# A pair of attention layers on one core: the final steps of two units on GpSimd, and the last unit in strided halves

## The reference

```python
for layer in (L0, L1):
    h = group_norm(x, 32 groups, eps) * gain + bias
    q, k, v = h @ Wq + bq, h @ Wk + bk, h @ Wv + bv     # 64 x 64 each, per position
    s = softmax((q @ k.T) * 64**-0.5)                   # 1024 x 1024 for each image
    x = x + (s @ v) @ Wo + bo
```

## Time and profile before

| what | us |
|---|---|
| time, median of 3 runs | 185.82 (185.78 to 186.77) |
| span of the profiled execution, first to last instruction | 184.0 |
| median less span, what lies around it | 1.8 |
| TensorE busy, share of the span | 174.6, 95% |
| VectorE | 138.3, 75% |
| GpSimd | 121.8, 66% |
| ScalarE | 100.4, 55% |

### The profile page before, as it was taken

How to read it: one execution, slowest core, us unless ns; L and a number is a source line. 1 busy time by engine, 2 the same in 40 slices (tenths; PEclk the granted TensorE clock), 3 DMA queues, 4 the chain that set the end, 5 groups by cost and what they waited for, 6 DMA issues and landing times.

```text
span 184.0 us, 3303 instructions
## 1 busy us (share of the span) xinstructions
PE 174.6 (95%) x1223; PEld 93.5 (51%) x1223; DVE 138.3 (75%) x208; ACT 100.4 (55%) x137; POOL 121.8 (66%) x81
## 2 busy tenths in 40 slices
PE   7778899999999999999999999999999999999993
PEld 4435545555525644455535645555535555456661
DVE  2799987779887687859875787769875588386763
ACT  3479367606656376436666476527656554466500
POOL 5265017996799929996699949996799939705000
PEclk9999999999999999999999999999999999999999
DMA  5544100500016000420025000500025100110111
GB/s 154 189 100 98 34 2 0 114 4 2 0 34 142 2 0 14 102 60 0 0 54 122 0 4 20 136 18 0 5 59 115 61 0 21 37 61 7 50 57 57
DMA packets 7103, 8.89 MB, mean 48 GB/s; under 512 B 1656, under 2 KB 4144, under 8 KB 7088
## 3 DMA queue, kind: packets, MB, share of 16 engines
q1 hardware_dynamic: 6080, 7.84, 16.9%
q10 hardware_dynamic: 1008, 0.86, 1.6%
HBM read 1.58 MB, written 1.05 MB: 14 GB/s over the span
## 4 chain that ended last, share of the span: by engine, by line
PE 82%; DVE 13%; DMA 1%; issue 1%; POOL 0%; ACT 0%; DVEq 0%; POOLq 0%
PE ps_attn L887 27%; PE ps_max L817 9%; DVE part_max L588 8%; PE ps_scores L855 8%; PE ps_scores L871 7%; PE ps_scores L857 7%; PE ps_scores L859 7%; PE ps_scores L796 3%; PE ps_misc L804 2%; PE ps_attn L894 2%; PE ps_misc L900 2%; DMA xs<-x_dram 1%; PE ps_misc L894 1%; DVE quarter_rden L628 1%; PE ps_misc L831 1%
## 5 line engine op out<-in xcount | busy, mean ns | idle before, releaser
L313 POOL TENSOR_TENSOR prob_sum<-prob_sum,probs 128x1024 f32<-128x1024 f32 x41 | 97.5, 2377 | 29.0 <-ACT probs L441 16.8
L588 DVE TENSOR_REDUCE part_max<-ps_max 128x2 f32<-128x1024 f32 x60 | 73.4, 1224 | 26.3 <-PE ps_max L818 25.8
L441 ACT ACTIVATE probs<-ps_scores 128x1024 f32<-128x1024 f32 x62 | 61.0, 1025 | 46.1 <-PE ps_scores L872 45.4
L887 PE MATMUL ps_attn<-probs,vals 128*64 128x512 f32 x224 | 54.5, 605 | 0.0
L887 PEld LDWEIGHTS ps_attn<-probs,vals 128*64 128x64 f32 x224 | 13.5, 136 | 27.8 <-issue 19.2
L871 PE MATMUL ps_scores<-q_row,ones_r 64*128 64x512 f32 x62 | 24.5, 396 | 0.5 <-ACT q_row L423 0.5
L872 PE MATMUL ps_scores<-q_row,ones_r 64*128 64x512 f32 x62 | 24.6, 396 | 0.0
L817 PE MATMUL ps_max<-back,front 64*128 64x512 f32 x31 | 13.9, 449 | 2.3 <-DVE part_max L588 1.4
L817 PE MATMUL ps_max<-cross,front 64*128 64x512 f32 x29 | 14.6, 505 | 0.3 <-DVE part_max L588 0.3
L818 PE MATMUL ps_max<-cross,back 64*128 64x512 f32 x29 | 14.6, 505 | 0.0
L818 PE MATMUL ps_max<-front,back 64*128 64x512 f32 x31 | 14.0, 450 | 0.0
(11 more groups left out here) (157 smaller groups left out, 365.7 us busy)
## 6 DMA issues: line engine op xcount, KB each, us to landing
cross<-front SPq DMA_DIRECT2D x16, 128.0 KB, 2.3
cross<-back SPq DMA_DIRECT2D x16, 128.0 KB, 2.3
rden<-quarter_rden SPq DMA_DIRECT2D x44, 32.0 KB, 1.8
xs<-x_dram SPq DMA_DIRECT2D x4, 256.0 KB, 4.6
out_dram<-xs SPq DMA_DIRECT2D x3, 256.0 KB, 2.0
rden<-quarter_rden ACTq DMA_DIRECT2D x12, 32.0 KB, 1.9
q_row<-max_rows SPq DMA_DIRECT2D x14, 2.0 KB
layer<-layers_dram SPq DMA_DIRECT2D x1, 194.5 KB, 2.7
```

Of the source, the lines that this page charges most:

```text
L313: pool.tensor_tensor(total[:, :], total[:, :], probs[t][:, :], ALU.add).then_inc(added, 1)
L441: act.activation(probs[t][:, :], scores_buffer(u, t)[:, :], ACT.Exp, scale=SCALE).then_inc(exp_done, 1)
L588: dve.tensor_reduce(part_max[u % 2][:, at:at + 2 * JS + 1:2 * JS], ps[:, :].rearrange("p (g n) -> p g n", g=2), AX.X, ALU.max, negate=True ...
L887: mm = pe.matmul(ps_attn[half * C:(half + 1) * C, :], v, probs[t][:, cols], start=(t == 0), stop=(t == TILES - 1))
```

## The change

It touches only the end of the program, in five places.

1. The final steps of units 5 and 6 become `finish` on GpSimd. Unit 5's comes behind tile 5 of unit 6, unit 6's at the very end of GpSimd's queue. The stores of those units wait for `final_done` instead of `tail_final`.
2. GpSimd adds tiles 2 and 3 of unit 7 (`TAIL_ADDS` is (4, 2)). VectorE collects the rest in `late_sum`: tile 4 plus tile 5, plus tile 6, plus `prob_sum`, plus tile 7. TensorE then sums one tile over its rows, one group in place of two.
3. The two halves of unit 7 are strided: half c takes every other block of 128 columns (`split`), not the first or second 256. With that, one reciprocal piece serves one half.
4. `spread_last` writes the two halves to different PSUM buffers and raises its semaphore for each; ScalarE copies each as its own instruction; the spread of both comes between `values_last(0)` and `values_last(1)`. ScalarE's copy waits for unit 6's multiply (`normed`), and `finish_last(0)` for unit 5's final step.
5. TensorE's order: `denominators(6)` comes one values tile earlier, values tile 7 of unit 6 behind score tile 3, values tile 1 of unit 7 behind the last score tiles, and values tile 4 ahead of the last sums.

```diff
-    TAIL_ADDS = (4, 1)
+    TAIL_ADDS = (4, 2)
...
+        def split(columns, c):
+            return columns.rearrange("p (k c n) -> p k c n", k=2, c=2)[:, :, c, :]
...
+        def last_rden(c):
+            return (ps_max, scores_buffer(LAST, TILES - 2))[c][:, 0:HALF // 2]
...
                 sp.wait_ge(quarter_done, 2 * u + 2)
-                if u == LAST - 1:
-                    sp.wait_ge(tail_normed, 1)
-                elif u:
+                if u:
                     sp.wait_ge(normed, u)
...
                 for t in range(2, 2 + pool_adds(w)):
                     add(w, t)
-                    if t == 5 and 0 < w < LAST - 1:
+                    if t == 5 and 0 < w < LAST:
                         finish(w - 1)
+            finish(LAST - 1)
...
-            act.wait_ge(last_spread, 1)
-            act.wait_ge(tail_normed, 2)
-            act.activation(rden[:, :], ps_max[:, HI], ACT.Copy).then_inc(last_rden, 1)
+            act.wait_ge(normed, LAST)
+            for c in range(2):
+                act.wait_ge(last_spread, c + 1)
+                act.activation(split(rden[:, :], c), last_rden(c), ACT.Copy).then_inc(last_copied, 1)
+            act.wait_ge(tail_final, 2)
+            act.dma_start(split(out[B - 1], 1), split(xs[:, slot(LAST + B)], 1)).then_inc(stored, 16)
...
+            def add_late(step):
+                if step == 1:
+                    dve.wait_ge(exp_done, TILES * LAST + 6)
+                    dve.wait_ge(tail_added, 1)
+                    first, second = probs[4], probs[5]
                 else:
+                    first, second = late_sum, (probs[6], prob_sum[LAST % 2], probs[7])[step - 2]
+                    dve.wait_ge(late_added, step - 1)
+                    if step == 3:
+                        dve.wait_ge(added, added_count(LAST, 3))
+                    else:
+                        dve.wait_ge(exp_done, TILES * LAST + (7 if step == 2 else 8))
+                dve.tensor_tensor(late_sum[:, :], first[:, :], second[:, :], ALU.add).then_inc(late_added, 1)
...
-            finish_tail(LAST - 2)
             pair_tail(LAST - 1)
             add_tail(LAST - 1)
             first_add(LAST)
             reciprocal(LAST - 1, 0)
             reciprocal(LAST - 1, 1)
-            for t in range(3, TILES - 1):
-                add_late(t)
-            finish_tail(LAST - 1)
+            for step in range(1, 5):
+                add_late(step)
...
-                pe.wait_ge(late_added, TILES - 4)
-                quarter_sums(ps_max[:, HALF:HALF + HALF // 2], prob_sum[LAST % 2], True, False)
-                pe.wait_ge(exp_done, TILES * UNITS)
-                quarter_sums(ps_max[:, HALF:HALF + HALF // 2], probs[TILES - 1], False, True).then_inc(den_mm, 1)
+                pe.wait_ge(late_added, 4)
+                quarter_sums(ps_max[:, HALF:HALF + HALF // 2], late_sum, True, True).then_inc(den_mm, 1)
...
             values(LAST - 1, 6)
-            values(LAST - 1, 7)
             pe.wait_ge(max_staged, UNITS)
             denominators(LAST - 1)
             scores(LAST, 3)
+            values(LAST - 1, 7)
             scores(LAST, 4)
             scores(LAST, 5)
             pe.wait_ge(quarter_done, 2 * LAST)
             values(LAST, 0)
-            values(LAST, 1)
             scores(LAST, 6)
             scores(LAST, 7)
+            values(LAST, 1)
             values(LAST, 2)
             values(LAST, 3)
+            values(LAST, 4)
             denominators_last()
-            values(LAST, 4)
             values(LAST, 5)
+            values_last(0)
             spread_last(0)
             spread_last(1)
-            values_last(0)
             values_last(1)
```

More of the change, by code:

```diff
@@ L250, in store @@
                 unit = UNITS - B + image
[L251 to L254, removed]
+                sp.wait_ge(final_done, unit + 1)
                 sp.dma_start(out[image], xs[:, slot(unit + B)]).then_inc(stored, 16)
             def store_last():
-                at = (LAST + B) * HALF
-                sp.wait_ge(tail_final, 3)
-                sp.dma_start(out[B - 1, :, 0:HALF // 2], xs[:, at:at + HALF // 2]).then_inc(stored, 16)
+                sp.wait_ge(tail_final, 1)
+                sp.dma_start(split(out[B - 1], 0), split(xs[:, slot(LAST + B)], 0)).then_inc(stored, 16)
             for u in range(2):
@@ L445, in copy_attn @@
                 if u >= 2:
[L446 to L449, removed]
+                    act.wait_ge(final_done, u - 1)
                 act.activation(attn[u % 2][:, :], ps_attn[:, :], ACT.Copy).then_inc(attn_copied, 1)
@@ L649, in add_tail @@
                 dve.tensor_tensor(total[:, :], total[:, :], late_sum[:, :], ALU.add).then_inc(tail_added, 1)
[L651 to L655, removed]
-                else:
-                    dve.wait_ge(late_added, t - 3)
-                dve.tensor_tensor(total[:, :], total[:, :], probs[t][:, :], ALU.add).then_inc(late_added, 1)
@@ L669, in finish_last @@
             def finish_last(c):
-                a, at = attn[LAST % 2], (LAST + B) * HALF
-                cols = slice(c * HALF // 2, (c + 1) * HALF // 2)
-                dve.wait_ge(last_rden, 1)
-                dve.wait_ge(tail_final, 1)
+                a = split(attn[LAST % 2][:, :], c)
+                dve.wait_ge(last_copied, c + 1)
                 dve.wait_ge(pv_mm, TILES * UNITS - 1 + c)
-                dve.tensor_tensor(a[:, cols], (ps_attn, ps_misc)[c][:, 0:HALF // 2], rden[:, cols], ALU.mult).then_inc(tail_normed, 1)
@@ L676, in finish_last @@
-                dve.wait_ge(tail_normed, 3 + c)
+                if c == 0:
+                    dve.wait_ge(final_done, LAST - 1)
+                values = (ps_attn, ps_misc)[c][:, 0:HALF // 2].rearrange("p (k n) -> p k n", k=2)
+                dve.tensor_tensor(a, values, split(rden[:, :], c), ALU.mult).then_inc(tail_normed, 1)
+                dve.wait_ge(tail_normed, 1 + c)
                 dve.wait_ge(x_biased, UNITS)
-                dve.tensor_tensor(xs[:, at + cols.start:at + cols.stop], a[:, cols],
-                                  xs[:, LAST * HALF + cols.start:LAST * HALF + cols.stop],
+                dve.tensor_tensor(split(xs[:, slot(LAST + B)], c), a, split(xs[:, slot(LAST)], c),
@@ L891, in half_values @@
             def half_values(t, v, c):
-                for half in range(2):
-                    at = half * HALF + c * HALF // 2
+                for half, cols in enumerate(halves()):
                     mm = pe.matmul((ps_attn, ps_misc)[c][half * C:(half + 1) * C, 0:HALF // 2], v,
-                                   probs[t][:, at:at + HALF // 2], start=(t == 0), stop=(t == TILES - 1))
+                                   split(probs[t][:, cols], c), start=(t == 0), stop=(t == TILES - 1))
                 return mm
@@ L930, in spread_last @@
                         q = 2 * n + k
-                        at = k * HALF // 2 + c * P
-                        mm = pe.matmul(ps_max[n * C:(n + 1) * C, at:at + P],
+                        mm = pe.matmul(last_rden(c)[n * C:(n + 1) * C, k * P:(k + 1) * P],
                                        pick[:, q * C:(q + 1) * C], quarter_rden[:, c * P:(c + 1) * P],
                                        start=True, stop=True)
-                if c:
-                    mm.then_inc(last_spread, 1)
+                mm.then_inc(last_spread, 1)
             def setup(n):
```

13 lines of the change are left out of this document (1 added, 12 removed).

## The result

The changed kernel took 190.56 us (median of 4 runs, 189.87 to 191.12) against 186.22 us of the kernel before in the same runs: 1.0231 times as long, 95% interval 1.0193 to 1.0268. The forecast was 188.1, the range ended at 188.9. A second series gave 189.92 against 186.34, ratio 1.0195 (1.0153 to 1.0238). The direction and the main mechanism were forecast; the rise, 4.3 us where 2.3 were forecast, was nearly double.

A forecast was written before the change was run, and what follows sets the result against it. TensorE's gapless last stretch and VectorE's finishing pairs were taken as the bound. End 181.72 us, plus 0.4 for the additions and 2.0 for GpSimd's hold, gave 184.1 against 181.83 (+2.3): forecast 188.1 us, range 185.9 to 188.9.

The forecast's parts named there:

- TensorE's work: TensorE's final stretch: one group of sums removed (0.43 us), one order change added (0.35 us), 0.08 to 0.10 us saved.
- VectorE's additions: Unit 7's four late additions: the fourth needs tile 7 and ends late, so TensorE's last sums wait 0.4 us.
- the switches of the new order: TensorE's order in units 6 and 7: one more change between scores and values, costing 0.35 us.
- GpSimd's steps: GpSimd's multiply and add of unit 6, due at 174.0 us, hold VectorE's third and fourth late additions; 2.0 us lost.
- step 2: Second of VectorE's four late additions for unit 7, running when GpSimd's multiply comes due, laid out at 173.1 to 174.3 us.
- Rivals 1 and 2: VectorE's late additions: first, only one is held, 187.1 us, chance 0.15; second, no contention with GpSimd, 186.1 us, chance 0.15.
- rival 3: TensorE's last sums: late_sum ready by 176.53 us, GpSimd holds nothing, so not slower; 185.7 us, chance 0.10.
- The strides, 0 for the stores: Last stores in 512-byte instead of 1 KB pieces: landing taken as unchanged, 0 us, at worst 1.7 us more.
- rival 4: Last stores: as forecast, but small pieces land 0.5 to 1 us later; 188.9 us, chance 0.05.

The follow-up runs named there:

- the pairs: Kernel storing x unchanged, without the computation; VectorE and GpSimd start one instruction each at one signal, ten pairs; GpSimd's addition 3.38 us beside VectorE's two-input one, 2.34 alone.
- the filler in the gap: Changed kernel plus four matmuls with unused results ahead of TensorE's last group of sums; 189.03 us, ratio 1.0149 to the kernel before.
- gated: Changed kernel with GpSimd's final step of unit 6 waiting for VectorE's fourth late addition; 187.50 us, ratio 1.0057 to the kernel before.
- reordered kernel: Changed kernel with GpSimd's unit 6 step held back, TensorE's old order of scores and values, and prob_sum added second; 186.28 us, ratio 0.9998 to the kernel before.
- block stores: On top of the reordered kernel, one transfer for each 128-column block of the last unit, two per queue; 186.17 us, ratio 1.0003 to the kernel before.

## Why the prediction was right and where it failed

**TensorE's work**: right, where the clock is full. The sums begin when VectorE's fourth addition ends, and the groups have the sizes of the earlier trace rows.

**VectorE's additions, 0.4 us late by themselves**: right; 0.43 in the run with the step held back. The wait and the switches of the new order (0.35 in the prediction) make 0.78; taking both back gave 0.77 in the traces and 1.2 in the medians.

**GpSimd's steps, 2.0 us**: right in place and size. The two additions took 0.95 longer each, 1.9; holding the step back gave them their 1.23 again. The hold works in the other direction too: GpSimd's L319 is 1.66 instead of 1.28, since step 2 was running when it came due, and in the pairs it is GpSimd that waits. The Trainium skill ("SBUF — State Buffer", section "SBUF: two separate sides") has the rule that whichever of the two starts first keeps the shared ports for its whole instruction; these rows agree with it in both directions. Rivals 1 and 2 fall by the same rows; rival 3 as well.

**The strides, 0 for the stores**: wrong. The step that failed is "I take 0, since the nearest row is the same store". It was not the same store: the new one has twice as many pieces, each half as long. It lands after 2.2 us instead of 1.7, and takes 0.66 us to issue instead of 0.36. That was rival 4, given 0.05; its 0.5 us alone would have left the time at 188.6, inside the range.

**What had no term at all**: the clock. What took the time out of the range is work at the lower clock, and the step that failed is the price of the gap. The prediction read that the clock was full in all slices and that TensorE had no gap, forecast a gap of 2.4 us, and priced it at its own length ("End: 181.72 + 2.4 = 184.1"). The gap came, 2.32 us. In one of the two traces of the changed kernel the matmuls behind it ran at 1.2 GHz and the stretch took 1.6 us more; in the other they ran at 2.4 GHz. With the filler in the gap no execution of four was at 0.991 or below, where nine of ten had been, and the median fell by 0.9 us. That this fall happens in most executions is inferred from those means, not seen in traces.

**The sum**: in the first trace 1.0 us at the start of the program, 2.3 for the additions and their wait and 0.5 for the stores make the 3.8 of the span. The 1.0 is a fall of the clock in a stretch that the change leaves alone, which nothing in the trace of the kernel before announced. The one execution with full clock has a span of 186.9 against 184.0, 2.9, where 2.3 + 0.5 = 2.8; that it fits to 0.1 is partly luck, since spans vary by more at full clock (183.7 to 184.8 in the kernel before). The medians of the two series differ by 4.3 and 3.6; the 1.5 and 0.8 that are over fit the clock, but no run splits them by execution.

Left open: in how many executions the clock fell at the start and in how many at the end, what the three at 0.987 had, whether the other 0.4 us between the gated and the reordered kernel is the clock, why one queue's block stores land at 2.1 and whole pieces once at 2.9, and why the first series is 0.6 us above the second.

## What to carry to other kernels

Before work is moved to GpSimd, look at what VectorE runs beside it at that moment: here two-input additions in SBUF and GpSimd's own took turns, and reciprocals from PSUM did not. Price a forecast gap on TensorE with the clock behind it, as a second case beside the gap's own length, and where a gap can't be closed, try to fill it. Price a store that is the last thing in a program by its pieces too, not only by its bytes: the 0.37 us by which the reordered kernel ended earlier on VectorE were eaten by its stores. And before a mean clock is blamed on a change, look in the trace where it fell; here one mean, 0.991, stood for two different places.

## What the runs showed of the hardware

A VectorE addition of two SBUF tiles (1.23 us) delayed GpSimd's addition by 1.04 us; a single-input VectorE instruction on float32 in SBUF, 1024 elements in 0.69 us, delayed it by 0.50. A GpSimd memset of 0.95 us beside a two-input addition delayed neither, and with one input in PSUM GpSimd's addition kept its 2.34 us. The delay shows in the records as a longer instruction (2.17 us for 1.23), not as idle time.

Behind a TensorE wait of 2.32 us the granted clock was 0.50 in one trace of the changed kernel and 1.00 in another; behind one of 0.43 us it was 1.00 in both traces that have it (the step held back, with strided and with whole stores).

A 128 KB store to HBM in 512-byte pieces took 2.2 to 2.3 us to land in six traces and 0.66 to 0.75 to issue. In 1 KB pieces it took 1.7 in two traces, 1.9 to 2.9 in two others, and 0.34 to 0.37 to issue.
